# A two-layer hybrid block on one core: maxima lead the scores by 26 chunks in place of 28, and a stack load is moved behind row loads

## The reference, cut to what matters

```python
x = x + attn_a(layernorm(x))     # 32 heads of 8, every query sees every key
x = x + ffn(layernorm(x))        # silu(x@w_gate) * (x@w_up), the 2 largest of each 4 kept, @w_down
x = x + attn_b(layernorm(x))     # 32 query heads, 8 key heads, j in [i-128, i) is masked out
x = x + ffn(layernorm(x))
# x: (2, 1024, 256) float32; both attentions: softmax(q k^T / sqrt(8)) v, then an output projection
```

## Time and profile before, and how to read it

| | us |
|---|---|
| median of three executions | 1705.37 |
| lowest and highest | 1704.73, 1710.11 |
| the profiled execution's own time | 1703.32 |
| its span, first to last instruction | 1701.5 |

### The profile page before, as it was taken

The page is one execution under the profiler, slowest core; times in us unless marked ns, Lnnn a source line. Parts: engine busy times, 40 slices in busy tenths (PEclk is TensorE's granted clock), DMA queues, the critical chain, the costliest instruction groups (busy, mean ns, idle before and its releaser), DMA issues.

```text
span 1701.5 us, 38923 instructions
## 1 busy us (share of the span) xinstructions
PE 1652.5 (97%) x13872; PEld 653.1 (38%) x13872; DVE 1470.9 (86%) x2144; ACT 1283.5 (75%) x2424; POOL 267.2 (16%) x623
## 2 busy tenths in 40 slices
PE   6899999999999999999988999999999999999999
PEld 4322222222222224776653222222222222247777
DVE  6999999999999992665767999999999999837655
ACT  3299999999999997333223999999999999963220
POOL 1410000000000000000012223333223333310000
PEclk9989999999999999999997999999999999999999
DMA  6954333345333312100405222233222222111000
GB/s 165 296 152 86 73 61 68 62 83 86 70 65 68 62 34 72 53 1 1 114 14 144 56 50 56 50 64 72 55 53 56 53 55 65 58 39 37 13 13 25
DMA packets 72126, 114.68 MB, mean 67 GB/s; under 512 B 12464, under 2 KB 27824, under 8 KB 71984
## 3 DMA queue, kind: packets, MB, share of 16 engines
q1 hardware_dynamic: 71984, 112.63, 28.7%
HBM read 71.96 MB, written 40.63 MB: 66 GB/s over the span
## 4 chain that ended last, share of the span: by engine, by line
PE 89%; DVE 4%; DMA 3%; ACT 2%; issue 2%; SPq 0%; POOL 0%; ACTq 0%; POOLq 0%; DVEq 0%
PE psum L742 32%; PE psum L724 20%; PE psum L800 13%; PE psum L694 12%; PE psum L822 6%; PE psum L657 2%; DVE mneg L1214 2%; PE psum L780 2%; DMA max_rows<-mT 1%; ACT area L988 1%; PE psum L677 1%; PE psum L639 1%; PE psum L712 1%; DVE xn L1220 1%; DMA area<-max_rows 0%
## 5 line engine op out<-in xcount | busy, mean ns | idle before, releaser
L988 ACT ACTIVATE area<-psum 128x512 f32<-128x512 f32 x2048 | 1099.6, 602 | 41.9 <-PE psum L724 16.0
L742 PE MATMUL psum<-area 128*32 128x256 f32 x8192 | 655.2, 392 | 0.6 <-POOL area L1469 0.4
L724 PE MATMUL psum<-area 51*128 51x512 bf16 x2048 | 639.5, 386 | 2.5 <-DMA area<-max_rows 1.4
L1220 DVE CUSTOM_DVE_ANT_0 xn<-psum,band 128x1024 f32<-128x1024 f32 x512 | 588.2, 1220 | 11.7 <-PE psum L694 11.2
L1214 DVE TENSOR_REDUCE mneg<-psum 128x1 f32<-128x1024 f32 x512 | 581.6, 1271 | 8.3 <-PE psum L694 7.9
L742 PEld LDWEIGHTS psum<-area 128*32 128x32 f32 x8192 | 162.1, 108 | 400.3 <-issue 262.5
L694 PE MATMUL psum<-area 48*128 48x512 bf16 x1024 | 301.7, 386 | 10.5 <-DVE mneg L1214 7.7
L724 PEld LDWEIGHTS psum<-area 51*128 51x128 bf16 x2048 | 142.7, 94 | 426.3 <-ACT area L988 353.3
L694 PE MATMUL psum<-k_max_b,area 48*128 48x512 bf16 x1024 | 291.1, 385 | 8.7 <-DVE mneg L1220 7.9
L1031 ACT ACTIVATE area<-psum 128x512 f32<-128x512 f32 x64 | 38.3, 598 | 159.7 <-PE psum L800 159.6
L1450 POOL TENSOR_TENSOR mparts<-mneg,nought 128x16 bf16<-128x16 f32 x64 | 14.1, 221 | 714.9 <-DVE mneg L1214 504.1
(11 more groups left out here) (74 smaller groups left out, 823.9 us busy)
## 6 DMA issues: line engine op xcount, KB each, us to landing
ctx_rows<-area SPq DMA_DIRECT2D x64, 256.0 KB, 3.6
area<-q_stacks SPq DMA_DIRECT2D x32, 384.0 KB, 7.1
area<-k_stacks SPq DMA_DIRECT2D x64, 192.0 KB, 5.6
area<-q_stacks_b SPq DMA_DIRECT2D x32, 384.0 KB, 5.4
area<-q_stacks SPq DMA_DIRECT2D x32, 192.0 KB, 4.4
area<-q_stacks_b SPq DMA_DIRECT2D x32, 192.0 KB, 3.3
area<-ctx_rows SPq DMA_DIRECT2D x16, 256.0 KB, 4.9
area<-inv_rows SPq DMA_DIRECT2D x16, 256.0 KB, 5.6
```

The source lines that it names most:

```text
L724: pe.matmul(psum[:, BANK_OF["exp", g, u, head], :], k_st[lo:lo + ROWS + PARTS, buf, 0 if a else head // 2, kt * P:(kt + 1) * P], q_st[lo:l ...
L742: mm = pe.matmul(psum[head * VW:(head + 1) * VW, BANK_OF["ctx", g, qh], cols], vaug[:, buf, kt, head, :], probs[:, u % PRING, head, cols], ...
L988: act.activation(probs[:, u % PRING, head, :], psum[:, BANK_OF["exp", like, u, head], :], ACT.Exp, scale=SCALE).then_inc(bank_freed, 1)
L1220: dve.tensor_tensor_reduce(band_out[:, c % 2, :], slot, band[:, at:at + SEQ], 1.0, -3.0e38, ALU.add, ALU.max, mneg[:, qh, col:col + 1]).th ...
```

## The change

`SHIFT` goes from 2 to 3 and `TURN` from 4 to 5, and with SHIFT `LEAD` from 28 to 26. On the SP queue `load_max_stack` for the group after next goes from ahead of the store of the context to behind `move_max` of half 1.

```diff
-SHIFT = 2
-TURN = 4
+SHIFT = 3
+TURN = 5
 LEAD = CHUNKS - 2 * SHIFT
...
             def group(a, g, buf, first=False, ahead=2, inverses=None):
                 if ahead >= 1:
                     load_st_stack(a, g + 1, 1 - buf)
-                if ahead >= 2:
-                    load_max_stack(a, g + 2, buf)
                 if not first:
                     store_ctx(a, g - 1, 1)
                 move_max(a, g, buf, 1)
+                if ahead >= 2:
+                    load_max_stack(a, g + 2, buf)
                 if first and a == 0:
                     load_late_weights()
                 store_ctx(a, g, 0)
```

## The result

| | before | after |
|---|---|---|
| median of five executions, us | 1710.04 | 1719.31 |
| lowest and highest, us | 1704.73, 1710.98 | 1715.05, 1722.35 |
| ratio of the times, 95% interval | | 1.0066 [1.0052, 1.0080] |
| the profiled execution's own time, us | 1703.32 | 1717.15 |
| its span, us | 1701.5 | 1715.2 |

The changed kernel is slower. The forecast was 1709.1 with 1714 as its upper end, so the median lies above all of it. Against executions of the kernel before on the same chip the change costs 0.66%, some 11 us, where the sum said 3.7. The busy shares of the page tell nothing of it: TensorE is again at 97%. The line that gives a hint is that of the scores, where 8.4 us of TensorE's idle time in front of L724 ended with a row load.

The account below looks back on a forecast made before the run. Steady groups were taken as narrowly bound by VectorE's maxima, shortened only at their ends. Terms +2.2 + 2.3 - 0.3 - 0.8 + 0.3 = +3.7 us on the 1705.37 median gave 1709.1 us, range 1703.8 to 1714.

Parts of the forecast that it names:

- What gates unit 0: Start of both attentions: row load (attention 0) and VectorE's copy of V (attention 1) release the first scores; saving 0.
- The rival of a shorter front: Unit 0 starts two chunks earlier in both attentions, 4.56 us off, 1704.5; either end alone 10%, with rows in time 5%.
- The last chunk a unit later: Last group of each attention: last chunk computed in unit 2 instead of 1, costing 2.27 us in attention 0, 2.29 in attention 1.
- the early units: Early units of attention 1 run at ScalarE's first exponentials, so two fewer chunks ahead may give back 0.3 us.
- The waits at unit 8: Last groups: TensorE waits for row loads behind the context loads, 2.1 us in attention 0 and 2.6 in attention 1.
- the unit that falls away: Last groups: five units instead of six to unit 8 after the last chunk; the saved unit is given back in waiting.
- The chain of attention 0: Last group of attention 0, from the last chunk through the SP queue to unit 8's scores: taken as 14.3 us.
- The relief of the moved load: Middle groups of attention 0: mT stores no longer behind maxima-stack loads, 0.8 us off, bounds 0 and 4.3.
- The rival of the store that is late for another reason: Half 1s of attention 0: score-stack loads hold mT up, stall up to 2.7 us each, up to 1752 us; 4%.
- The weights' collision: Group 0 of attention 0: moved load meets the late weights, 0.3 us, bounds 0 and 3; at bound 1712.9, 10%.
- The clock: Rival: waits at unit 8 and the pause before unit 0 halve TensorE's clock, about +3 us each, 1712 or 1715; 14%.

Follow-up runs that it names:

- experiment 9: Kernel before (SHIFT 2, TURN 4, LEAD 28) with the moved load outside attention 0's first group and the last groups' context loads split around the move; 1703.89 us, ratio 0.9980.
- experiment 10: Changed kernel (lead 26) with maxima-stack loads ahead in attention 0's first group and the last groups' context loads split around the move; 1704.70 us, ratio 0.9985.
- experiment 1: Changed kernel, but in the last groups four of the eight context loads go behind the move of half 1's maxima; 1709.61 us, ratio 1.0014 to before.
- experiment 6: Changed kernel, but in attention 0's first group the maxima-stack loads stay ahead of the move; 1712.28 us, ratio 1.0029 to before.
- experiment 4: Changed kernel with the load order of before (SHIFT 3, TURN 5, maxima-stack loads ahead of store and move); 1746.26 us, ratio 1.0243 to before.
- experiment 3: Kernel before with the moved load alone (SHIFT 2, TURN 4); 1707.62 us, ratio 0.9999 to before.
- experiment 5: Changed kernel with three extra float32 matmuls, results unused, ahead of unit 8 of both last groups; 1714.47 us, ratio 1.0035 to before.
- 2: Changed kernel, but the late weights are issued behind the move of the next group's half 0; 1714.62 us, ratio 1.0044 to before.
- 7: Changed kernel with the four parts of attention 1's last V projection one chunk earlier each; 1721.69 us, ratio 1.0077 to before.
- 8: Changed kernel with first-group maxima-stack loads ahead, last groups' context loads split around the move, and attention 1's V a chunk earlier; 1703.18 us, ratio 0.9968 to before.

## Why the prediction was right and wrong

- **What gates unit 0: right.** Saving 0 in both attentions, the releasers as named, 3.3 us of idle time in front of the first. The rival of a shorter front is out.
- **The last chunk a unit later: right.** It shows clean in attention 1, 559.47 - 557.25 = 2.2 us for 2.29, and between experiments 9 and 10, 2.35. The 0.3 taken off for the early units did not come.
- **The waits at unit 8: right in place and size** (2.58 and 2.48 for 2.1 and 2.6), as was the reading that they eat the unit that falls away: experiment 1 gets it back. The chain of attention 0 was 15.04 us, not 14.3, 0.7 more.
- **The relief of the moved load: right.** 0.6 from experiment 6, 1.4 from experiment 10, 1.5 from experiment 9 (552.16 - 550.64), for 0.8. The rival of the store that is late for another reason is out as far as the change goes, and experiment 4 shows what it would have looked like.
- **The weights' collision: the step that failed first.** I had taken 0.3 with 3 as its bound, "the queue having mostly emptied in time". It measured 5.9. The times behind it were right: the queue empty near 120 to 123 and the store out at 117 (122.3 and 116.78). The value drawn from them was not. A store issued 5.5 us before the weights are in waits for most of them, which gives a stall at the upper bound, 2.9 us, and I had taken the lower end. And the term had no place for the clock: another 3.0 us came behind the stall.
- **The clock: named as a rival, and priced too low in chance.** "It decides from a gap somewhat longer than 2.8 us" rested on one gap that had left the clock at full. Gaps of 2.91, 2.58 and 2.48 us all lowered it. I had given 14% to what happened in three places. The size, about 3 for each, was near (3.0, 2.5 and 1.4). The Trainium skill ("TensorE: Matmul & The Clock Gate", Why this matters for your kernels) warns of idle gaps between matmul bursts that drop the clock, but from a length a little above all three of these. The trace agrees that such gaps lower the clock, and shows it for shorter ones than the page names; there the measurement decides.

The sum again, in the terms of the forecast and against the profiled spans: 3.7, plus 5.6 for the collision with its clock (5.9 for 0.3), plus 2.5 and 1.4 for the clock in the last groups, plus 0.7 and less 0.2 for their chains, plus 0.2 and 0.2 for relief and early units that were smaller, less 0.6 at the edges of the stages: 13.5 of the 13.7 us. Of the ten missing ones 6.9 (3.0, 2.5 and 1.4) are the clock behind a gap and 2.6 the gap of the collision (2.9 for 0.3).

## What to carry to other kernels

Price a new stall of TensorE twice, once for its length and once for the matmuls behind it at half clock, unless the trace shows several gaps of that length that leave the clock alone. When a load is moved on a queue, follow it to the one place where other bulk transfers are in flight, and compare the issue of each small store with the landing of what is ahead, not with its issue. When a change shifts work from one side of a critical transfer to the other, look first for whether the transfer is in time: here that decided all, and the lead nothing.

## What was not expected of the hardware

**The same gap does not always have the same effect on the clock.** Between the two attentions TensorE waits 2.84 us for a copy of weights by VectorE. After the change, in timeline and windows:

```profile
824.28 1.96 PE L657 MATMUL psum<-xnT,wqo_b 128*128 128x512 f32 x4 [2.84 <-DVE wqkvo L1182]
```

```profile
825.00:835.00 10.00, 10.00 (x48) 7.87 (x47) 7.86 (x15) 2.31 (x4) 0.00 (x0) 1.00 0.71 218
```

and in experiment 3, where none of the code of this stage is changed either:

```profile
814.81 2.46 PE L657 MATMUL psum<-xnT,wqo_b 128*128 128x512 f32 x4 [2.84 <-DVE wqkvo L1182]
```

```profile
816.00:826.00 10.00, 10.00 (x37) 8.19 (x36) 6.79 (x12) 1.72 (x3) 0.00 (x0) 0.51 0.74 224
```

The clock is 1.00 in the one and 0.51 in the other, and the stage takes 250.28 and 253.50 us. Of the twelve profiled executions, before, after and experiments 5 and 6 had no fall there and took 248.3 to 250.3 us for the stage; 2, 4, 7 and 8 had one of three or four us and took 249.8 to 251.8; 1, 3, 9 and 10 had one of some ten us and took 253.4 to 253.5. The two lowest, 248.3 in 5 and 249.8 in 4, lack another fall of this stage, which before and after have behind a pause of 1.68 us. So a gap that a single trace shows as harmless is a gap whose effect varies, and a part of the spread between executions of one kernel (6.3 us for the one before) is of that size; that the spread comes from there was not tested.

**A wait of 1.22 us was followed by a fall as well.** It stands in all twelve executions, in attention 1, where a reciprocal of VectorE (L1229) comes between two maxima. The clock stayed at 1.00 behind it in eight of them; in experiments 4, 7, 8 and 10 it fell for four to eight us. In attention 0 the same reciprocal gives TensorE a wait of 1.06 to 1.19 us, and the clock fell behind it in experiments 5, 7 and 8. Why it falls in some executions and not in others was not settled.

**The slow stretch behind the first scores of attention 1 differs in length too.** It lasts eleven us in before, after and experiments 1, 2, 3 and 6, some fourteen in 7 to 10, and eighteen in 4 and 5. The windows after the change and in experiment 5:

```profile
931.00:942.00 11.00, 9.22 (x44) 1.93 (x44) 7.94 (x14) 7.48 (x13) 2.91 (x5) 0.53 1.06 308
928.00:946.00 18.00, 15.71 (x84) 3.01 (x88) 12.27 (x21) 11.03 (x20) 5.72 (x13) 0.53 0.72 202
```

The groups of attention 1 took 562.28 us in experiment 5 with no fall behind the 1.22 us wait, against 559.47 after the change. So the 564.35, 564.38 and 562.29 us of experiments 7, 8 and 10 are not the price of that wait alone.

**A small store behind bulk loads takes their time, not its own:** 12 KB landed after 1.4 us alone, after 4.3 to 6.0 us behind the stack loads of attention 0 in the kernel before, and after 6.1 to 6.6 us behind stack loads and weights together (after the change and in experiments 1, 3, 5 and 7).
